# Normalized rows of an attention layer: transposed on TensorE, or loaded channel-major and normalized on GpSimd

## The chip, the cores and the metric

The kernel runs on one core of one Trainium2 chip. The metric is the time of the whole kernel on the device in microseconds (us). The engines are TensorE (PE in the profile), VectorE (DVE), ScalarE (ACT), GpSimd (POOL) and SyncE (SP, which here only starts DMAs). Each works through its own list of instructions in order and waits on semaphores for the others.

## The reference, cut to what matters

Input `x` is 128 batch items of 128 tokens by 384 channels, `adj` is 128 x 128 per item. Two layers follow each other:

```python
x = x + gnn(layernorm(x), adj, adj, ...)     # layer A: 12 heads of 32 channels
x = x + ffn(layernorm(x), ...)               # layer B: 3 heads of 128 channels

# layer A
q, k, v = h @ Wq.T, h @ Wk.T, h @ Wv.T + bv              # h = layernorm(x)
scores = q k^T * scale + 2 * adj                         # per head; rows all zero are masked
out = softmax(scores) @ v @ Wo.T + bo

# layer B
gate = softmax(relu(h @ Wg1 + bg1) @ Wg2 + bg2)          # two best of three, softmax again
q, k, v per head; q of head 0 passes a convolution over tokens (3 taps)
out = (causal softmax attention per head, weighted by the gate) @ Wp + bp
```

`layernorm(x)` is (x - mean) / sqrt(var + 1e-5) over the 384 channels of a token. The result must come close to float32, so the kernel splits each operand of the large products into two float16 parts (`hi` and `lo`) and adds three products per operand pair.

## The kernel before

The 128 items are worked in 32 groups of 4. In the main loop a *turn* holds one group of layer A (from its scores on), one group of layer B (the group before that), and, "ahead", the normalized rows and q, k of the group that layer A takes in the next turn. The turn is the same from turn 2 to turn 31. Turns 0 and 1 and the last groups have lists of their own (`FIRST_STEPS`, `LAST_STEPS`).

The order on each engine is a table, `ORDER_OF_STEPS`: for each engine a list of steps such as `A.score.1.2` (layer A, item 1, block 2 of four heads). Each engine runs its steps strictly in that order; semaphores hold the engines to each other. The steps that matter here:

- `A.ln1`: DVE computes mean and variance of the next group's rows (L807, L811), POOL turns them into -mean and 1/sqrt(var) (L1048 to L1051) and normalizes the 4 items into `h1`, tokens on partitions (L1054).
- `A.hT.c` (c = 0, 1, 2): PE transposes block c of 128 channels of the 4 items into one PSUM bank (four transposes, L560), ACT writes the float16 `hi` part from it (L677), DVE the `lo` part (L927). `A.qk.0` needs all three blocks.
- `A.score` (PE, then DVE L957, then ACT exp L712), `A.norm` (DVE row factors L974 to L982, then POOL L1096), `A.turn` (PE transposes the probabilities, ACT copies them, L726), `A.mix`, `A.proj`: layer A's attention.
- `B.qk.c` (ACT evacuates it, L701 or L704), `B.v`, `B.score`, `B.norm`, `B.turn`, `B.mix`, `B.proj`: layer B. `B.score.0` waits until ACT has evacuated `B.qk.5`.
- `B.gate.0`, `.1`, `.2`: the gate on DVE (L873 to L899), with two small exponentials on ACT (L735) between the parts. `B.gate.0` has five instructions with two inputs in SBUF: three of L875, L879, L882.
- `A.res`, `B.res`: POOL adds a bias row to the residual (L1082, L1091).
- `A.stack.0`, `.1`: SP copies q and k parts to `Qs` and `Ks` with 24 DMAs (L492). The first waits for the last scores of the group before; the next turn's first scores wait for the last.

PSUM has 8 banks: 5 used in rotation by layer A's steps, 3 by layer B's. A step on PE waits until the step that used its bank before has been evacuated.

Of the kernel before, what the change touches and what calls it, by code (L numbers as in the profile page):

```python
# [45 lines left out]
GB = 4  # L46
# [80 lines left out]
        A.score.0.0 A.score.0.1 A.v.0 A.v.1 A.score.0.2 B.hT.0 B.hT.1 B.hT.2 A.score.1.0 A.score.1.1 A.v.2  # L127
        B.qk.0 B.v.0 B.v.1 A.score.1.2 B.qk.1 B.v.2 A.turn.0.0 A.v.3 A.turn.0.1 B.v.3 B.qk.2 A.turn.0.2 B.qk.3
        A.hT.0 A.score.2.0 A.hT.1 A.mix.0 A.score.2.1 B.qk.4 A.hT.2 B.qk.5 A.turn.1.0 A.proj.0 B.score.0
        A.turn.1.1 B.score.1 A.score.2.2 A.qk.0 A.turn.1.2 A.score.3.0 A.qk.1 A.qk.2 A.qk.3 B.turn.0 A.qk.4  # L130
        B.mix.0 A.score.3.1 A.mix.1 A.score.3.2 B.turn.1 B.score.2 A.turn.2.0 A.qk.5 A.turn.2.1 A.proj.1
# [5 lines left out]
        A.score.1.1 A.turn.0.2 B.qk.2 A.hT.0 A.score.1.2 A.hT.1 B.gate.0 A.mix.0 B.qk.3 A.hT.2 B.qk.4 B.qk.5
        A.turn.1.0 A.score.2.0 A.turn.1.1 A.score.2.1 A.qk.0 B.gate.1 B.score.0 A.qk.1 A.turn.1.2 A.score.2.2
        B.score.1 A.qk.2 B.turn.0 A.qk.3 A.qk.4 A.score.3.0 B.mix.0 A.mix.1 B.turn.1 A.turn.2.0 A.score.3.1
        B.score.2 A.score.3.2 A.turn.2.1 A.turn.2.2 B.mix.1 A.qk.5 A.mix.2 B.turn.2 B.score.3 A.turn.3.0 B.mix.2  # L140
        A.turn.3.1 A.turn.3.2 B.turn.3 A.mix.3 B.mix.3
    """,
    "dve": """
        A.score.0.0 A.v.0 A.score.0.1 A.score.0.2 B.hT.0 B.hT.1 B.hT.2 A.smax.0 A.v.1 A.score.1.0 B.v.0 A.norm.0
        A.score.1.1 A.ln1 A.v.2 B.v.1 A.score.1.2 B.v.2 A.v.3 B.conv B.v.3 A.smax.1 B.gate.0 A.hT.0 A.norm.1
        A.hT.1 A.score.2.0 A.mix.0 A.hT.2 A.score.2.1 B.gate.1 B.score.0 A.proj.0 A.score.2.2 B.score.1 B.gate.2
        A.qk.0 B.norm.0 A.smax.2 A.qk.1 A.score.3.0 B.norm.1 A.norm.2 A.qk.2 A.qk.3 A.qk.4 A.score.3.1 A.mix.1
        B.score.2 A.score.3.2 B.mix.0 A.smax.3 B.norm.2 A.norm.3 B.score.3 B.mix.1 A.qk.5 A.proj.1 B.proj.0
# [1020 lines left out]
```

## Time and profile before

| what | us |
|---|---|
| three runs, median (lowest to highest) | 2238.28 (2237.51 to 2238.32) |
| the profiled execution, whole time | 2238.38 |
| its span, first to last instruction | 2236.3 |
| PE busy in the span | 2201.6 (98%) |
| DVE busy | 1903.9 (85%) |
| ACT busy | 1500.0 (67%) |
| POOL busy | 1157.3 (52%) |

Engines work at the same time, so their busy times don't add up. A time is bound by the engine that is never idle, or by a circle of waits; the share tells the first, the waits the second.

### The profile page before, as it was taken

To read this page: it belongs to the slowest core of one execution; us is meant where nothing else is said; L and a number is where in the kernel's file an instruction comes from. 1 tells how busy PE (TensorE), PEld (TensorE's weight loads), DVE (VectorE), ACT (ScalarE), POOL (GpSimd) and SP (SyncE) were. 2 spreads that over 40 slices of the span, in tenths; PEclk is the share of its full clock that TensorE was granted. 3 is DMA by queue.
4 is the path that set the end of the run, shared out by engine and by line. 5 is a ranking of instruction groups with operands and counts; after the bars stand their busy time and mean duration, and the time that the engine had idled before them with its cause. 6 is when DMAs were issued, how large, how long until landed. Compare 5 with 4: busy or idle time off the path is not lost.

```text
span 2236.3 us, 51593 instructions
## 1 busy us (share of the span) xinstructions
PE 2201.6 (98%) x16941; PEld 1439.2 (64%) x16941; DVE 1903.9 (85%) x7152; ACT 1500.0 (67%) x5298; POOL 1157.3 (52%) x1551
## 2 busy tenths in 40 slices
...
DMA packets 142265, 143.20 MB, mean 64 GB/s; under 512 B 16816, under 2 KB 141360, under 8 KB 142000
## 3 DMA queue, kind: packets, MB, share of 16 engines
...
q8 instruction: 137, 2.24, 0.4%
...
q14 instruction: 128, 1.05, 0.2%
...
## 4 chain that ended last, share of the span: by engine, by line
PE 94%; DVE 2%; SPq 1%; POOL 1%; issue 1%; DMA 0%; ACT 0%; DVEq 0%; POOLq 0%
PE B_bank L517 33%; PE A_bank L517 32%; PE A_bank L597 7%; PE A_bank L609 4%; PE B_bank L616 4%; PE A_bank L584 4%; PE B_bank L591 4%; PE B_bank L601 2%; PE A_bank L560 2%; PE B_bank L560 2%; SPq L492 1%; DVE raw_score L957 1%; DVE smax L963 0%; DMA Ks<-k_hi 0%; POOL S L1096 0%
## 5 line engine op out<-in xcount | busy, mean ns | idle before, releaser
L712 ACT ACTIVATE S<-raw_score,smin 128x128 f32<-128x128 f32 x1536 | 593.9, 393 | 172.9 <-DVE smin L957 172.9
L1096 POOL TENSOR_TENSOR S<-S,rowf 128x512 f32<-128x512 f32 x384 | 389.1, 1041 | 314.8 <-DVE rowf L982 314.8
L957 DVE CUSTOM_DVE_ANT_0 raw_score<-A_bank,adj,s_unit 128x128 f32<-128x128 f32 x1536 | 444.7, 346 | 4.3 <-PE A_bank L584 1.5
L1101 POOL TENSOR_TENSOR S<-S,row2f 128x384 f32<-128x384 f32 x128 | 106.0, 828 | 612.1 <-DVE row2f L990 611.9
L726 ACT ACTIVATE PT<-A_bank 128x512 f32<-128x512 f32 x384 | 220.1, 590 | 234.9 <-PE A_bank L597 234.9
L712 ACT ACTIVATION_READ_ACCUMULATOR S<-raw_score,smin 128x1 f32 x1536 | 296.0, 193 | 0.0
L597 PE MATMUL A_bank<-ident,S 128*128 128x128 f32 x1536 | 226.7, 274 | 3.6 <-DVE smin L957 2.5
L963 DVE TENSOR_REDUCE smax<-raw_score 128x12 f32<-128x1536 f32 x128 | 223.0, 1742 | 0.0
L597 PEld LDWEIGHTS A_bank<-ident,S 128*128 128x128 f32 x1536 | 187.0, 141 | 41.4 <-DVE smin L957 3.4
L719 ACT ACTIVATE S<-S,s2min 128x128 f32<-128x128 f32 x384 | 148.4, 390 | 3.0 <-DVE s2min L967 3.0
L584 PE MATMUL A_bank<-Ks,Qs 96*128 96x128 f16 x1536 | 140.6, 221 | 7.7 <-DMA Ks<-k_hi 5.0
L584 PEld LDWEIGHTS A_bank<-Ks,Qs 96*128 96x128 f16 x1536 | 109.1, 98 | 37.1 <-issue 12.1
L517 PE MATMUL B_bank<-wv2g_hi,b_hT_hi 128*128 128x416 f16 x384 | 130.2, 339 | 1.0 <-DVE V L946 1.0
L517 PE MATMUL B_bank<-wv2g_lo,b_hT_hi 128*128 128x416 f16 x384 | 130.2, 339 | 0.0
L517 PE MATMUL B_bank<-wv2g_hi,b_hT_lo 128*128 128x416 f16 x384 | 130.2, 339 | 0.0
L957 DVE DVE_READ_ACCUMULATOR2_ANT smin<- 128x1 f32 x1536 | 127.4, 83 | 0.0
L1091 POOL TENSOR_TENSOR x1res<-x,bp_row 128x384 f32<-128x384 f32 x128 | 125.4, 1008 | 3.0 <-DMA out<-x1res 3.0
L517 PE MATMUL A_bank<-wo_hi,oT_hi 128*128 128x384 f16 x384 | 125.2, 326 | 1.8 <-DVE oT_lo L938 1.8
L517 PE MATMUL B_bank<-wp_hi,yT_hi 128*128 128x384 f16 x384 | 125.2, 326 | 1.6 <-DVE yT_lo L938 1.5
L1082 POOL TENSOR_TENSOR xres<-xin,bo_row 128x384 f32<-128x384 f32 x128 | 125.7, 1015 | 0.0
L517 PE MATMUL A_bank<-wv_hi,a_hT_hi 128*128 128x384 f16 x384 | 125.3, 326 | 0.0
L517 PE MATMUL B_bank<-wp_hi,yT_lo 128*128 128x384 f16 x384 | 125.2, 326 | 0.0
(192 smaller groups left out, 6155.8 us busy)
## 6 DMA issues: line engine op xcount, KB each, us to landing
xin<-in_x SPq DMA_DIRECT2D x32, 768.0 KB, 4.5
...
out<-x1res SPq DMA_DIRECT2D x128, 192.0 KB, 2.1
...
Qs<-q_lo SPq DMA_DIRECT2D x128, 96.0 KB, 2.2
Ks<-k_lo SPq DMA_DIRECT2D x126, 96.0 KB, 2.3
...
```

Of the source, the lines that this page charges most:

```text
L517: mm = nc.tensor.matmul(dst, left(c)[a], right(c)[b], start=(c == 0 and n == 0), stop=(c == KC - 1 and n == 2))
L584: mm = nc.tensor.matmul(dst[:, tok(j)], Qs[:, c * HPC + j, tok(b)], Ks[:, c * HPC + j, tok(b)], start=True, stop=True)
L597: mm = nc.tensor.transpose(dst[:, tok(j)], S[b % 2][:, c * HPC + j, :], ident[:])
L712: ins = nc.scalar.activation(S[b % 2][:, h, :], raw_score[:, h, :], ACT.Exp, bias=smin[b % 2][:, h:h + 1], scale=-1.0, accum_out=ssum[b % ...
L719: ins = nc.scalar.activation(S2[b % 2][:, e, :], S2[b % 2][:, e, :], ACT.Exp, bias=s2min[b % 2][:, e:e + 1], scale=-1.0, accum_out=s2sum[b ...
L726: nc.scalar.activation(dst, src[:, 0:dst.shape[1]], ACT.Copy).then_inc(evacuated[stage, "act"], 1)
L957: ins = nc.vector.tensor_tensor_reduce(raw_score[:, h, :], src[:, j * T:(j + 1) * T], adj2[:, b, :], s_unit[:], 3.0e38, ALU.add, ALU.min, ...
L963: nc.vector.tensor_reduce(smax[b % 2][:], raw_score[:], AXX, ALU.max).then_inc(maxed, 1)
L1082: nc.gpsimd.tensor_tensor(xres[:, b, :], xin[:, b, :], bo_row[:], ALU.add).then_inc(xres_ready, 1)
L1091: nc.gpsimd.tensor_tensor(x1res[:, b, :], x1[:, b, :], bp_row[:], ALU.add).then_inc(x1res_ready, 1)
L1096: nc.gpsimd.tensor_tensor(S[b % 2][:, hs, :], S[b % 2][:, hs, :], rowf[b % 2][:, hs].unsqueeze(2).broadcast_to([P, HPC, T]), ALU.mult).the ...
L1101: nc.gpsimd.tensor_tensor(S2[b % 2][:], S2[b % 2][:], row2f[b % 2][:].unsqueeze(2).broadcast_to([P, NE, T]), ALU.mult).then_inc(normed2, 1)
```

## The change

The host hands over a second copy of `x`, already channel-major (`xT`: group, channel in block, block, item and token). From group 2 on (`TURNED`):

- SP loads a group's `xT` into `xt` (`A.xT`, 768 KB). `xt` takes the place of `h1`.
- POOL computes -mean and 1/sqrt(var) as before (now `A.ln1` is only that), but these lie one token per partition. SP writes them to DRAM as rows (`A.stat`: 128 partitions x 8 values, each of 4 bytes to a place of its own) and reads them back to all 128 partitions (`A.rows`: `stat_wide`, 128 x 1024).
- POOL normalizes block c with two instructions of 128 x 512 (`A.hx.c`): add -mean, multiply by 1/sqrt(var).
- ACT and DVE read `xt` in SBUF instead of a PSUM bank to write the `hi` and `lo` parts. PE has no `A.hT` steps.

Groups 0 and 1 are transposed as before. The tables of the main loop are new for all five engines.

```diff
+                if (stage, kind) == ("A", "xT") and not last:
+                    if following(g) == TURNED:
+                        wait_products(sp, ("A", "hT", KC - 1, 0), g)
+                    else:
+                        wait_evacuated(sp, ("A", "hT", KC - 1, 0), g)
+                    sp.dma_start(xt[:], xT[following(g)]).then_inc(xT_loaded, 16)
+                if (stage, kind) == ("A", "stat"):
+                    sp.wait_ge(rstd1_done, count(g, 1, 1))
+                    sp.dma_start(stat_rows[g].rearrange("q b t -> t q b"), stat[g % 2][:],
+                                 allow_slow_non_contiguous=True).then_inc(stat_stored, 16)
+                if (stage, kind) == ("A", "rows"):
+                    sp.wait_ge(stat_stored, count(g - TURNED, 16, 16))
+                    if g > TURNED:
+                        sp.wait_ge(hx_ready, count(g - TURNED, KC, 0))
+                    sp.dma_start(stat_wide[:], stat_rows[g].rearrange("q b t -> q (b t)").unsqueeze(0)
+                                 .broadcast_to([P, 2, GB * T])).then_inc(stat_spread, 16)
...
+                elif kind == "hT" and A and g >= TURNED:
+                    act.wait_ge(hx_ready, count(g - TURNED, KC, b + 1))
+                    if b == 0:
+                        wait_products(act, ("A", "v", GB - 1, 0), before(g))
+                        wait_products(act, ("A", "qk", 2 * KC - 1, 0), before(g))
+                    nc.scalar.activation(hT_hi["A"][:, b, :], xt[:, b, :], ACT.Copy, scale=H_SCALE)\
+                        .then_inc(hi_ready["ahead"], 1)
...
-                    nc.vector.scalar_tensor_tensor(out=hT_lo[stage][:, b, :], in0=src[:, :], scalar=H_SCALE,
+                    rows_T = xt[:, b, :] if turned(step, g) else src[:, :]
+                    nc.vector.scalar_tensor_tensor(out=hT_lo[stage][:, b, :], in0=rows_T, scalar=H_SCALE,
...
+                elif kind == "hx":
+                    if b == 0:
+                        pool.wait_ge(xT_loaded, count(g - TURNED, 16, 16))
+                        pool.wait_ge(stat_spread, count(g - TURNED, 16, 16))
+                    nc.gpsimd.tensor_tensor(xt[:, b, :], xt[:, b, :], stat_wide[:, 0, :], ALU.add).then_inc(centred, 1)
+                    pool.wait_ge(centred, count(g - TURNED, KC, b + 1))
+                    nc.gpsimd.tensor_tensor(xt[:, b, :], xt[:, b, :], stat_wide[:, 1, :],
+                                            ALU.mult).then_inc(hx_ready, 1)
```

Of the new tables, PE's up to `A.qk.0` and POOL's:

```diff
     "pe": """
+        A.score.0.0 A.v.0 A.score.0.1 A.v.1 A.score.0.2 A.score.1.0 B.hT.0 B.hT.1 B.hT.2 A.v.2 B.qk.0
+        A.score.1.1 A.score.1.2 B.qk.1 B.v.0 A.turn.0.0 A.turn.0.1 B.v.1 B.qk.2 A.turn.0.2 B.v.2 A.mix.0 A.v.3
+        B.v.3 A.score.2.0 B.qk.3 A.turn.1.0 A.turn.1.1 A.score.2.1 A.turn.1.2 B.qk.4 B.qk.5 A.score.2.2 A.proj.0
+        B.score.0 A.mix.1 B.score.1 A.qk.0 A.qk.1 A.score.3.0 A.qk.2 A.qk.3 B.turn.0 A.score.3.1 B.score.2
...
     "pool": """
+        A.res.0 A.res.1 A.res.2 A.res.3 B.res.0 A.norm.0 A.ln1 A.norm.1 B.res.1 A.hx.0 A.hx.1 A.hx.2 B.norm.0
+        A.norm.2 B.norm.1 B.res.2 B.norm.2 A.norm.3 B.res.3 B.norm.3 A.ln2.0 A.ln2.1 A.adj A.ln2.2 A.ln2.3
```

POOL's list in a turn, from the residual rows of layer A to the norm of layer B's first item, before:

```order
L1082 TENSOR_TENSOR xres<-xin,bo_row 128x384 x4
L1096 TENSOR_TENSOR S<-S,rowf 128x512 x3
L1048 TENSOR_SCALAR nmean<-mv 128x4
L1049 TENSOR_SCALAR ve<-mv 128x4
L1051 TENSOR_TENSOR rstd<-ve,half 128x4
L1054 TENSOR_SCALAR h<-xin,nmean,rstd 128x384 x4
L1091 TENSOR_TENSOR x1res<-x,bp_row 128x384 x4
```

The same stretch now:

```order
L1138 TENSOR_TENSOR S<-S,rowf 128x512 x3
L1133 TENSOR_TENSOR x1res<-x,bp_row 128x384
L1168 TENSOR_TENSOR xt<-xt,stat_wide 128x512
L1170 TENSOR_TENSOR xt<-xt,stat_wide 128x512
L1168 TENSOR_TENSOR xt<-xt,stat_wide 128x512
L1170 TENSOR_TENSOR xt<-xt,stat_wide 128x512
L1168 TENSOR_TENSOR xt<-xt,stat_wide 128x512
L1170 TENSOR_TENSOR xt<-xt,stat_wide 128x512
L1143 TENSOR_TENSOR S<-S,row2f 128x384
```

Before, four normalizations (L1054) and four residual rows (L1091) stood in one run, ahead of `A.norm.1`. Now `A.norm.1` (L1138 x3) and one residual row come first, and then the six `A.hx` instructions in one run, ahead of `B.norm.0`.

ACT's list in the middle of a turn, where the gate's first exponential (L735) stands, before:

```order
L677 ACTIVATE a_hT_hi<-A_bank 128x512
L712 ACTIVATE S,ssum<-raw_score,smin 128x128 x4
L677 ACTIVATE a_hT_hi<-A_bank 128x512
L735 ACTIVATE g_tmp<-g_tmp 128x12
L730 ACTIVATE oT_hi<-A_bank 128x384
L704 ACTIVATE k<-B_bank,bqk_col,hinv 128x512
L677 ACTIVATE a_hT_hi<-A_bank 128x512
L704 ACTIVATE k<-B_bank,bqk_col,hinv 128x512 x2
```

The same stretch now (the gate's exponential is L769):

```order
L746 ACTIVATE S,ssum<-raw_score,smin 128x128 x4
L769 ACTIVATE g_tmp<-g_tmp 128x12
L707 ACTIVATE a_hT_hi<-xt 128x512
L738 ACTIVATE k<-B_bank,bqk_col,hinv 128x512
L760 ACTIVATE PT<-A_bank 128x512 x2
L738 ACTIVATE k<-B_bank,bqk_col,hinv 128x512
L746 ACTIVATE S,ssum<-raw_score,smin 128x128 x4
L707 ACTIVATE a_hT_hi<-xt 128x512 x2
```

Two evacuations of `B.qk` (L738), `.4` and `.5`, and two of `A.turn.1` (L760) now stand behind both the gate's exponential and the first block of `A.hT`.

DVE's list there now, from the last two `B.v` to the first block of `A.hT`; each `ISA` row is one of four alike:

```order
L981 SCALAR_TENSOR_TENSOR V<-B_bank,v_unit,bvg_row 128x416 x2
L992 ISA raw_score,smin<-A_bank,adj,s_unit 128x128
...
L907 TENSOR_SCALAR g_hid<-V 128x128
L909 TENSOR_TENSOR q2raw<-g_hid,wg_row 128x128 x3
L912 TENSOR_REDUCE g_tmp<-q2raw 128x12
L913 TENSOR_TENSOR g_tmp<-g_tmp,bg_row 128x12
L914 TENSOR_REDUCE g_col<-g_tmp 128x4
L916 TENSOR_TENSOR g_tmp<-g_tmp,g_col 128x12
...
L962 SCALAR_TENSOR_TENSOR a_hT_lo<-xt,a_hT_hi 128x512
```

`B.gate.0` (L907 to L916) has the same instructions as before; it follows `A.score.2.0` now, where it followed `A.smax.1`, and the two-input form of `A.hT` (L962) comes behind it, later in the list.

## Rows read from the trace of the kernel before

**Rows 1.** The page: span; part 1: busy us, share, instructions.

```profile
span 2236.3 us, 51593 instructions
PE 2201.6 (98%) x16941; PEld 1439.2 (64%) x16941; DVE 1903.9 (85%) x7152; ACT 1500.0 (67%) x5298; POOL 1157.3 (52%) x1551
```

**Rows 2.** Windows: one turn; PE, PEld, DVE, ACT, POOL busy; PEclk.

```profile
607.19:675.36 68.17, 68.17 (x530) 44.68 (x528) 58.86 (x223) 46.36 (x166) 35.67 (x48) 1.00 0.24 63
```

**Rows 3.** Chain of waits by time: start, us, engine, tile, matmuls.

```profile
638.13 1.32 PE B_bank L560 x12
646.47 0.23 PE A_bank L584 x4
650.66 1.46 PE A_bank L517 x9
652.56 3.52 PE B_bank L517 x18
...
658.46 0.44 PE A_bank L560 x4
659.57 0.79 PE A_bank L609 x24
...
671.52 5.83 PE A_bank L517 x27
```

**Rows 4.** Timeline of PE and POOL: start, us, instruction.

```profile
634.37 0.61 PE L584 MATMUL A_bank<-Ks,Qs 96*128 96x128 f16 x8
...
650.35 1.04 POOL L1051 TENSOR_TENSOR rstd<-ve,half 128x4 f32<-128x4 f32 x1
```

**Rows 5.** Groups by line, POOL: busy us, mean ns | idle before.

```profile
L1096 POOL TENSOR_TENSOR S<-S,rowf 128x512 f32<-128x512 f32 x384 | 389.1, 1041 | 314.8 <-DVE rowf L982 314.8
L1082 POOL TENSOR_TENSOR xres<-xin,bo_row 128x384 f32<-128x384 f32 x128 | 125.7, 1015 | 0.0
L1054 POOL TENSOR_SCALAR h<-xin,nmean,rstd 128x384 f32<-128x384 f32 x126 | 112.2, 902 | 3.5
```

**Rows 6.** Lines L875 and L979: min/median/max ns, first and last start.

```profile
L875 DVE TENSOR_TENSOR q2raw<-g_hid,wg_row x9: 278/991/1082, 657.1 to 795.4; 128x128 f32<-128x128 f32 x9
L979 DVE SCALAR_TENSOR_TENSOR live<-smax,live x128: 105/107/671, 52.2 to 2173.7; 128x12 f32<-128x12 f32 x128
```

**Rows 7.** Timeline of POOL, then DVE, around the gate's first part.

```profile
655.03 3.92 POOL L1091 TENSOR_TENSOR x1res<-x,bp_row 128x384 f32<-128x384 f32 x4
...
657.10 2.20 DVE L875 TENSOR_TENSOR q2raw<-g_hid,wg_row 128x128 f32<-128x128 f32 x3
...
660.33 0.17 DVE L882 TENSOR_TENSOR g_tmp<-g_tmp,g_col 128x12 f32<-128x12 f32 x1
```

**Rows 8.** Groups by line, ACT and DVE.

```profile
L712 ACT ACTIVATE S<-raw_score,smin 128x128 f32<-128x128 f32 x1536 | 593.9, 393 | 172.9 <-DVE smin L957 172.9
L726 ACT ACTIVATE PT<-A_bank 128x512 f32<-128x512 f32 x384 | 220.1, 590 | 234.9 <-PE A_bank L597 234.9
L704 ACT ACTIVATE k<-B_bank,bqk_col,hinv 128x512 f32<-128x512 f32 x96 | 74.1, 773 | 24.0 <-PE B_bank L517 24.0
L677 ACT ACTIVATE a_hT_hi<-A_bank 128x512 f16<-128x512 f32 x96 | 56.5, 589 | 54.4 <-PE A_bank L560 54.4
...
L957 DVE CUSTOM_DVE_ANT_0 raw_score<-A_bank,adj,s_unit 128x128 f32<-128x128 f32 x1536 | 444.7, 346 | 4.3 <-PE A_bank L584 1.5 <-DVE smax L963 0.3
L946 DVE SCALAR_TENSOR_TENSOR V<-B_bank,v_unit,bvg_row 128x416 f32<-128x416 f32 x128 | 82.4, 644 | 19.4 <-PE B_bank L517 19.4
```

**Rows 9.** Timeline of SP, another turn: start, us of issuing.

```profile
1158.93 6.43 SPq L492 DMA_DIRECT2D Qs<-q_hi  x8
...
1173.83 3.99 SPq L492 DMA_DIRECT2D Ks<-k_hi  x4
```

**Rows 10.** Part 6 of the page: KB each, us to landing.

```profile
xin<-in_x SPq DMA_DIRECT2D x32, 768.0 KB, 4.5
...
out<-x1res SPq DMA_DIRECT2D x128, 192.0 KB, 2.1
```

More of the change, by code:

```diff
@@ L126 @@
     "pe": """
[L127 to L131, printed above, removed]
@@ L137 @@
[L137 to L141, printed above, removed]
+        A.score.0.0 B.hT.0 B.hT.1 B.hT.2 A.score.0.1 A.score.0.2 B.qk.0 A.score.1.0 B.qk.1 A.turn.0.0 A.turn.0.1
@@ new lines @@
+        A.score.1.1 A.turn.0.2 B.qk.2 A.score.1.2 A.mix.0 A.turn.1.0 B.qk.3 A.score.2.0 B.gate.0 A.hT.0 B.qk.4
+        A.turn.1.1 A.turn.1.2 B.qk.5 A.score.2.1 A.hT.1 A.hT.2 A.mix.1 B.gate.1 B.score.0 A.qk.0 A.qk.1
+        A.score.2.2 B.score.1 B.turn.0 A.qk.2 A.qk.3 A.score.3.0 B.mix.0 A.turn.2.0 B.score.2 A.score.3.1 A.qk.4
+        A.score.3.2 B.turn.1 A.turn.2.1 A.qk.5 A.turn.2.2 B.mix.1 B.turn.2 B.score.3 A.turn.3.0 A.mix.2
+        A.turn.3.1 A.turn.3.2 B.mix.2 A.mix.3 B.turn.3 B.mix.3
@@ L142 @@
     """,
     "dve": """
[L144 to L148, printed above, removed]
@@ L149 @@
-        A.mix.2 B.norm.3 A.ln2.0 B.proj.1 A.ln2.1 B.mix.2 A.proj.2 A.mix.3 A.ln2.2 B.mix.3 B.proj.2 A.proj.3
-        A.ln2.3 B.proj.3
+        A.score.0.0 A.v.0 A.score.0.1 A.v.1 A.score.0.2 B.hT.0 B.hT.1 B.hT.2 A.smax.0 A.v.2 A.norm.0 A.score.1.0
+        A.ln1 A.score.1.1 A.score.1.2 B.v.0 B.v.1 A.smax.1 B.conv A.norm.1 A.mix.0 A.v.3 B.v.2 B.v.3 A.score.2.0
+        B.gate.0 A.score.2.1 B.gate.1 A.score.2.2 A.hT.0 A.proj.0 A.hT.1 A.hT.2 B.score.0 B.gate.2 A.mix.1
+        A.smax.2 B.score.1 B.norm.0 A.qk.0 A.norm.2 A.qk.1 A.score.3.0 A.qk.2 B.score.2 A.qk.3 B.norm.1
@@ L151 @@
+        A.score.3.1 A.score.3.2 B.norm.2 B.mix.0 A.smax.3 A.qk.4 A.norm.3 B.score.3 A.qk.5 B.proj.0 B.mix.1
+        A.proj.1 B.norm.3 A.ln2.0 A.mix.2 B.mix.2 A.ln2.1 B.proj.1 A.mix.3 A.proj.2 A.ln2.2 B.mix.3 A.proj.3
+        A.ln2.3 B.proj.2 B.proj.3
     """,
     "pool": """
-        A.res.0 A.res.1 A.res.2 A.res.3 A.norm.0 A.ln1 B.res.0 B.res.1 B.res.2 B.res.3 A.norm.1 B.norm.0
-        B.norm.1 A.norm.2 B.norm.2 A.norm.3 B.norm.3 A.ln2.0 A.ln2.1 A.adj A.ln2.2 A.ln2.3
+        A.res.0 A.res.1 A.res.2 A.res.3 B.res.0 A.norm.0 A.ln1 A.norm.1 B.res.1 A.hx.0 A.hx.1 A.hx.2 B.norm.0
@@ L206, with turned @@
 }
+def turned(step, g):
+    return step[:2] == ("A", "hT") and g >= TURNED
 def parse(word):
```

61 lines of the change are left out of this document (38 added, 23 removed).

## The prediction, written before the changed kernel was run

> **What bounds the kernel now.** I read the page's busy shares first: PE 98%, the next engine 85% [rows 1]. Then windows one turn long: in a window of 68.17 us PE is busy for 68.17 us at the full granted clock (2.4 GHz), DVE for 58.86, ACT for 46.36, POOL for 35.67 [rows 2]. So in a turn the time is what PE issues, and only less PE work, or a new wait of PE, can change it. The chain of waits says the same: it is one PE step behind another.
>
> **What goes.** Three A.hT steps a turn. In the chain one of them (four transposes) moves PE on by 0.44 us [rows 3]. They go for groups 2 to 31, 30 turns: 3 x 0.44 = 1.32 us a turn, 39.6 us in all. POOL loses four normalizations of 0.90 us a turn [rows 5], 3.6 us, off the path, since POOL is 52% busy [rows 1].
>
> **What comes, away from the path.** POOL gets six two-input instructions of 128 x 512 a turn. The trace has no such form with two full operands. Nearest rows: 1.04 us for 512 elements with a broadcast operand, 1.01 us for 384 elements with full operands [rows 5], which go at a step of 3.92 / 4 = 0.98 us [rows 7]. Scaled to 512 elements that is 1.31 us. Below: 1.04 + 0.1 for the own semaphore between the two of a block, 1.15. Above: 1.35 + 0.1 = 1.45. I take 1.3, so a block of 7.8 us. POOL's load rises by 4 us to about 40 of 68 us: it is not the bound. ACT and DVE keep their three A.hT instructions each, from SBUF instead of PSUM; I price them as before, 0.59 us on ACT [rows 8].
>
> **The new order, laid out.** I add up PE's steps from the turn's first score. Step costs: scores 0.23, B.hT all three 1.32, A.v and A.proj 1.46, qk 5.83 / 3 = 1.94, B.v 3.52 - 1.94 = 1.58, A.turn 0.44 (four transposes, as A.hT), A.mix 0.79 and 0.1 in front of it [rows 3]. Up to B.score.0 the new list has 9 scores, 4 A.v, B.hT, 6 B.qk, 4 B.v, 6 A.turn, one A.mix, one A.proj: 2.07 + 5.84 + 1.32 + 11.64 + 6.32 + 2.64 + 0.89 + 1.46 = 32.2 us. B.v.3 ends at 22.9, the third A.turn.0 at 17.3, A.qk.0 starts at 34.4 (B.score.0, A.mix.1 and B.score.1 add 2.2). These are the times if PE never waits.
>
> *When POOL starts the block.* ACT copies A.turn.0.2 (0.59), evacuates B.qk.2 (0.77) and does the four exponentials of A.score.1.2 (4 x 0.39) [rows 8]; less overlaps that is 17.5 to 20.3. DVE needs about 0.5 for the row factors (four short instructions, L979 is 0.11 when alone [rows 6]), POOL 3 x 1.0 for A.norm.1 and 1.0 for a residual row [rows 5]: the first A.hx can start at 25.0.
>
> *When DVE does the gate.* B.v.3 read from 23.1, 0.6 us; A.score.2.0, four of 0.35 that overlap, 1.1 us [rows 8]: B.gate.0 starts at 24.7. It took from 656.7, just ahead of 657.10, to 660.50 before [rows 7], 3.8 us. It would end at 28.5.
>
> So the gate's first part and the six A.hx run side by side, and that is the point of this prediction. L875 takes 278 ns at the least and 991 in the middle of nine [rows 6]. In the timeline POOL works through four L1091 until 658.95, and the three L875 that began at 657.10 took 2.20 us: each ended with a POOL instruction, only the third, when POOL was done, was short [rows 7]. L979, 105 ns, has been 671 [rows 6]. A DVE instruction with two SBUF inputs is held until POOL's running instruction ends. [...] Without such a rule this layout would give the clean case below; with it, what follows.
>
> B.gate.0 has five such instructions. They can each get in only at the end of an A.hx: ends at 26.3, 27.6, 28.9, 30.2, 31.5. So B.gate.0 ends at 31.7 instead of 28.5. ACT stands at the gate's exponential, and behind it in its list are A.hT.0, B.qk.4, two A.turn.1, B.qk.5: 0.59 + 0.77 + 2 x 0.59 + 0.77 = 3.3 us by the means [rows 8], about 3.0 as they overlap. B.qk.5 is evacuated at 34.7. PE wants B.score.0 at 32.2 and waits 2.5 us. Without the holds it would be 31.5, ahead of 32.2 by 0.7. A.qk.0 then comes at 36.9 and finds its first blocks (DVE reaches A.hT.0 near 35.5, having done A.score.2.1, the gate's second part and A.score.2.2); little is added there.
>
> Bounds of this wait: with 1.15 us an instruction the fifth end is at 30.8, less overlap on ACT, wait 1.5; with 1.45 it is 32.3, wait 3.2. If the block starts later than 25.0, the first part of the gate goes free, but its second part and A.hT.1 and .2 meet the block, which ends later itself: from a start at 28.5 it ends at 36.3, ACT and DVE add 1.3, and A.qk.0 wants its last block at 35.7: a wait of about 2. So it doesn't vanish by a shift.
>
> **The moments' way.** -mean and 1/sqrt(var) were ready 17.0 us into a turn (650.35 + 1.04 against 634.37 [rows 4]); A.ln1 now stands ahead of A.score.1.1 on DVE, so some 2 us earlier, 15. Until 25.0 there are 10 us for two dependent DMAs. A store of 192 KB lands in 2.1 us, a load of 768 KB in 4.5 [rows 10]. For the 1024 values of 4 bytes no row exists: below 2.1, above twice the 4.5 (xin is 512 pieces, this is 1024), 9. With 4.5 for the way back the pair takes 6.6 to 13.5; I take 9, hidden. The loads and SP's part in them lie far from the stacking in time.
>
> **The stacking.** The Q and K copies start when PE has done A.score.3.2 and must have landed before the next turn's first score. In a turn that is slow at it they took from 1158.93 to 1177.82 to issue [rows 9], 18.9 us (the longest of the 13 turns that I read; the shortest took 16.8), and some 1.5 to land (2.1 from the start of an issue, as for the stores [rows 10]). PE's list had 20.9 us between the two, now 19.8. A wait of up to 0.7 us in the slowest turns, two of those 13: 3 us over all, counted in.
>
> **Sum.** The profiled execution took 2238.38 us (span 2236.3, 2.1 around it), 0.1 above the median of the runs, so I count from 2238. A turn: -1.32 + 2.5 = +1.2 us. Thirty turns: +35. Stacking +3. Forecast 2276 us, slower. Its own range: 30 x (1.5 - 1.32) = +5 to 30 x (3.2 - 1.32) + 3 = +59: 2243 to 2298.
>
> **Rivals.**
> - *Clean.* The gate and the block don't meet as I laid them, or the lists have slack that I don't see, and PE stays 100% busy: 2238 - 39.6 + 3 = 2201 us, faster. For it: in the turn before, DVE was held by 1.4 us in the same gate and PE never waited [rows 2, 7]. Against it: that had some microseconds of other ACT work between, now ACT stands right behind the gate and PE's margin is 0.7. It decides at this point: if five holds cost less than 0.7 us together.
> - *Half.* The holds cost 1 to 1.5 us beyond the margin less what later steps win back: 30 x (1.2 - 1.32) = -4, 2220 to 2243 us. For it: my layout has an error of some tenths at each engine.
> - *The moments come late.* The 4-byte stores pass 10 us with the read. Each microsecond past it is a microsecond a turn once the wait for A.hT.2 leads: at 15 us for the pair the block starts at 30, ends at 37.8, its last block is ready at 39.1 against 35.7: +3.4 - 1.32 a turn, 2300; at 20 us 2450. For it, the Trainium skill (DMA: Bandwidth & Descriptors, "Specifications") wants 512 B and more for the full rate and has smaller pieces read, changed and written back; no row here has pieces of 4 bytes in number. Against: it is 4 KB in all over 16 DMA engines.
>
> **Chances.** Forecast 0.50, clean 0.33, half 0.10, late moments 0.07. What can be told from no change is about 0.2%, 4.5 us. Of half, 0.03 is faster by more than that, 0.01 slower by more, 0.06 within. So slower 0.50 + 0.07 + 0.01 = 0.58, faster 0.33 + 0.03 = 0.36, within 0.06. The range for 8 in 10 must hold the clean case too: 2198 to 2298.
>
> **What would show it.** In the changed profile, a window of one turn: PE's busy time near 67 in a turn of 69.4 (forecast) or of 66.9 (clean). PE's longest waits: B_bank of B.score.0, released by ACT's evacuation into k (forecast), or a_hT_lo from DVE or the stat_wide load (late moments). L909 (L875 before) with a median near 1.3 us and L913, L916 far above their 0.17: holds. The A.hx pair at 1.15 to 1.45 us each. ACT idle in front of the gate's exponential by about 3 us. Wrong at the root: L909 short, or the six A.hx finished before or begun after the gate, with PE fully busy.

## The result, and the profile after

The changed kernel took 2322.23 us, the median of four runs (2320.09 to 2324.97), against 2238.30 of the kernel before on the same chip (2237.51 to 2240.0): a ratio of 1.0375, interval 1.0357 to 1.0393. The profiled execution took 2324.97 us. So it is slower, as forecast, but by 84 us where 38 were forecast, and outside the range of 2198 to 2298.

The page of the changed kernel, its span, part 1 and the start of part 4 (the chain's shares); it answers to [rows 1]:

```profile
span 2323.2 us, 51084 instructions
...
PE 2210.8 (95%) x16581; PEld 1418.0 (61%) x16581; DVE 1899.8 (82%) x7152; ACT 1488.3 (64%) x5298; POOL 1285.9 (55%) x1611
...
PE 49%; DMA 18%; DVE 17%; POOL 6%; issue 5%; ACT 4%; SPq 1%; ACTq 0%; DVEq 0%; POOLq 0%
```

PE has 360 matmuls fewer and is busy 9 us longer than in [rows 1]. Of the chain, DMA now has 18%. The waits of the changed kernel (engine, tile and line waiting <- releaser: us in total, times, longest):

```profile
POOL xt L1168 <- DMA stat_wide<-stat_rows: 122.9, 30, 5.4
ACT a_hT_hi L707 <- POOL xt L1170: 110.8, 60, 4.5
...
PE B_bank L618 <- ACT k L738: 75.3, 31, 3.8
```

PE's wait stands exactly where it was forecast, at B.score.0 behind ACT's evacuation of B.qk.5, and its size, 75.3 / 30 = 2.5 us a turn, is the forecast's. Its cause is another. The timeline of one turn, which starts at 736.10 (SP's DMA issues, POOL and ACT, start and us; idle time before an instruction in brackets):

```profile
749.66 1.04 POOL L1090 TENSOR_TENSOR stat<-ve,half 128x4 f32<-128x4 f32 x1
750.73 0.38 SPq L498 DMA_DIRECT2D stat_rows<-stat  x1
...
761.00 0.34 SPq L505 DMA_DIRECT2D stat_wide<-stat_rows  x1
...
764.09 0.21 ACT L769 ACTIVATE g_tmp<-g_tmp 128x12 f32<-128x12 f32 x1
...
765.34 1.27 POOL L1168 TENSOR_TENSOR xt<-xt,stat_wide 128x512 f32<-128x512 f32 x1 [4.62 <-DMA stat_wide<-stat_rows]
...
767.98 0.63 ACT L707 ACTIVATE a_hT_hi<-xt 128x512 f16<-128x512 f32 x1 [3.69 <-POOL xt L1170]
...
770.14 0.79 ACT L738 ACTIVATE k<-B_bank,bqk_col,hinv 128x512 f32<-128x512 f32 x1
...
771.02 0.91 PE L618 MATMUL B_bank<-k,q 128*128 128x128 f32 x6 [3.00 <-ACT k L738]
```

The moments are ready 14.6 us into the turn. The store is issued at once, and the spread, which waits for it, only 10.3 us later; it lands after 4.2 us more. Over all 30 turns the first step takes 8.2 to 11.2 us (median 10.0) and the second 3.4 to 5.3 (median 4.5). POOL was free at 24.6 and starts the block at 29.2. ACT has done the gate's exponential at 764.3 and stands in front of A.hT.0 until the first block is done; B.qk.4 and B.qk.5 are queued behind it, and PE waits for the latter (the L738 row at 770.14).

The gate's first part had slipped through ahead of the block. L909, its three products, and L921, an instruction of the gate's second part (min/median/max ns; L909 answers to L875 in [rows 6]):

```profile
L909 DVE TENSOR_TENSOR q2raw<-g_hid,wg_row x96: 278/285/1121, 117.0 to 2293.4; 128x128 f32<-128x128 f32 x96
...
L921 DVE TENSOR_TENSOR g_tmp<-g_tmp,g_col x32: 170/809/1266, 120.9 to 2299.2; 128x12 f32<-128x12 f32 x32
```

L909 at a median of 285 ns is free; the second part, beside the block now, is held (L921, a median of 809 ns against 170 at the least). And there is a second cost. Windows of the same turn (start:end, length, busy of PE, PEld, DVE, ACT and POOL with instructions, granted clock, DMA share, GB/s), then the 4 us behind a wait of 2.91 us in the turn before and behind one of 1.98 us in the turn after:

```profile
736.10:807.87 71.77, 68.77 (x518) 44.02 (x517) 57.75 (x223) 45.99 (x165) 40.00 (x51) 0.98 0.29 78
768.00:771.00 3.00, 0.03 (x1) 0.01 (x1) 1.60 (x2) 3.00 (x6) 2.92 (x3) 1.00 0.00 0
771.00:773.00 2.00, 1.98 (x31) 1.50 (x31) 0.00 (x0) 1.97 (x9) 1.92 (x2) 0.85 0.00 0
773.00:775.00 2.00, 2.00 (x8) 1.52 (x9) 1.85 (x5) 1.11 (x3) 0.43 (x1) 0.50 0.00 0
775.00:777.00 2.00, 2.00 (x9) 0.80 (x8) 1.79 (x13) 1.26 (x6) 0.00 (x0) 0.80 0.00 0
...
698.00:702.00 4.00, 4.00 (x34) 3.33 (x35) 1.87 (x5) 3.17 (x12) 2.33 (x2) 0.50 0.00 0
841.80:845.80 4.00, 3.98 (x43) 2.57 (x44) 1.91 (x5) 3.02 (x12) 2.34 (x2) 1.00 0.00 0
```

Behind 22 of the 30 waits at B.score.0 the granted clock is 0.50 to 0.67 over the next 4 us, which is some microseconds at the 1.2 GHz level, and the matmuls take up to twice their time; behind the other 8 it is 1.00. PE is busy 68.77 us in the turn shown, where the layout had 66.9.

### The profile page after: what moved, and what is told of

Its sections match the earlier page's. It is cut to its first block, busy times and chain, and to the rows that moved or that the text cites. A ratio compares the mean times of both kernels' runs of the same rounds, so it can differ in the third digit from the quotient of the medians.

```text
span 2323.2 us, 51084 instructions
## 1 busy us (share of the span) xinstructions
PE 2210.8 (95%) x16581; PEld 1418.0 (61%) x16581; DVE 1899.8 (82%) x7152; ACT 1488.3 (64%) x5298; POOL 1285.9 (55%) x1611
## 4 chain that ended last, share of the span: by engine, by line
PE 49%; DMA 18%; DVE 17%; POOL 6%; issue 5%; ACT 4%; SPq 1%; ACTq 0%; DVEq 0%; POOLq 0%
PE A_bank L544 22%; DMA stat_rows<-stat 11%; PE B_bank L544 8%; DVE raw_score L992 6%; DMA stat_wide<-stat_rows 6%; PE B_bank L618 5%; PE A_bank L624 4%; PE B_bank L643 4%; PE A_bank L636 4%; DVE smax L998 3%; DVE bn L841 2%; DVE b_hT_lo L962 2%; ACT k L738 2%; PE B_bank L628 2%; POOL xt L1170 2%
## 5 line engine op out<-in xcount | busy, mean ns | idle before, releaser
L1138 POOL TENSOR_TENSOR S<-S,rowf 128x512 f32<-128x512 f32 x384 | 389.5, 1043 | 456.4 <-DVE rowf L1017 456.4
L992 DVE CUSTOM_DVE_ANT_0 raw_score<-A_bank,adj,s_unit 128x128 f32<-128x128 f32 x1536 | 439.6, 345 | 15.1 <-PE A_bank L611 14.5
L760 ACT ACTIVATE PT<-A_bank 128x512 f32<-128x512 f32 x384 | 217.6, 592 | 234.3 <-PE A_bank L624 234.3
L746 ACT ACTIVATION_READ_ACCUMULATOR S<-raw_score,smin 128x1 f32 x1536 | 301.9, 197 | 0.0
L624 PE MATMUL A_bank<-ident,S 128*128 128x128 f32 x1536 | 218.7, 275 | 3.6 <-DVE smin L992 2.5
L618 PE MATMUL B_bank<-k,q 128*128 128x128 f32 x768 | 132.6, 316 | 75.3 <-ACT k L738 75.3
L624 PEld LDWEIGHTS A_bank<-ident,S 128*128 128x128 f32 x1536 | 179.4, 142 | 36.3 <-issue 8.5
L1168 POOL TENSOR_TENSOR xt<-xt,stat_wide 128x512 f32<-128x512 f32 x90 | 114.5, 1272 | 122.9 <-DMA stat_wide<-stat_rows 122.9
L618 PEld LDWEIGHTS B_bank<-k,q 128*128 128x128 f32 x768 | 111.8, 219 | 97.0 <-ACT k L738 86.5
L962 DVE SCALAR_TENSOR_TENSOR a_hT_lo<-xt,a_hT_hi 128x512 f16<-128x512 f32 x90 | 75.9, 843 | 97.4 <-ACT a_hT_hi L707 93.2
L1170 POOL TENSOR_TENSOR xt<-xt,stat_wide 128x512 f32<-128x512 f32 x90 | 124.4, 1382 | 7.1
L707 ACT ACTIVATE a_hT_hi<-xt 128x512 f16<-128x512 f32 x90 | 56.6, 629 | 110.8 <-POOL xt L1170 110.8
```

The source lines that it names most:

```text
L618: mm = nc.tensor.matmul(dst[:, tok(e)], q2[:, e, tok(b)], k2[:, e, tok(b)], start=True, stop=True)
L624: mm = nc.tensor.transpose(dst[:, tok(j)], S[b % 2][:, c * HPC + j, :], ident[:])
L746: ins = nc.scalar.activation(S[b % 2][:, h, :], raw_score[:, h, :], ACT.Exp, bias=smin[b % 2][:, h:h + 1], scale=-1.0, accum_out=ssum[b % ...
L760: nc.scalar.activation(dst, src[:, 0:dst.shape[1]], ACT.Copy).then_inc(evacuated[stage, "act"], 1)
L992: ins = nc.vector.tensor_tensor_reduce(raw_score[:, h, :], src[:, j * T:(j + 1) * T], adj2[:, b, :], s_unit[:], 3.0e38, ALU.add, ALU.min, ...
L1138: nc.gpsimd.tensor_tensor(S[b % 2][:, hs, :], S[b % 2][:, hs, :], rowf[b % 2][:, hs].unsqueeze(2).broadcast_to([P, HPC, T]), ALU.mult).the ...
```

## The experiments

Eleven kernels ran. All times are against the kernel before on the same chip (2237.8 to 2238.5). The runs "no store", "narrow", "both" and "half" leave out part of the computation, as the text recorded ahead of each says, and show only what the time would be; the others compute the whole.

**The moments early: no store.**

```diff
-  sp.dma_start(stat_rows[g].rearrange("q b t -> t q b"), stat[g % 2][:], ...).then_inc(stat_stored, 16)
-  sp.wait_ge(stat_stored, count(g - TURNED, 16, 16))
-  sp.dma_start(stat_wide[:], stat_rows[g]. ...)
+  sp.dma_start(stat_wide[:], x[g * GB].rearrange("t c -> (t c)")[0:2 * GB * T]. ...)
```

> Left out: the store of the moments to DRAM; the load into stat_wide reads as many bytes of x instead, so layer A's rows are not normalized rightly. The load is issued when 1/sqrt(var) is done, 14.6 us into a turn, and lands at about 19, so the A.hx block starts when POOL is free, 24.7 to 25. Theory L (the lateness of the moments made the 2.4 us wait and the block itself is harmless): PE's wait at B.score.0 is gone and the time is the clean case, about 2201 us. Theory H (my forecast: the block held the five two-input instructions of B.gate.0): now the block really runs beside gate.0 and the wait is 2.5 us by the holds, the median of L909 near 1.1 us, time about 2276 us. In between (2215 to 2255) both have a part.

Measured: 2246.6 us, ratio 1.0034 (1.0020 to 1.0049). Neither theory alone. PE's longest wait:

```profile
PE B_bank L616 <- ACT k L736: 37.8, 31, 1.6
```

The gate's products, ns:

```profile
L907 DVE TENSOR_TENSOR q2raw<-g_hid,wg_row x96: 276/1261/1362, 114.2 to 2214.1; 128x128 f32<-128x128 f32 x96
```

And the timeline of POOL, DVE, ACT and PE in a turn from 705.99:

```profile
730.73 0.35 DVE L905 TENSOR_SCALAR g_hid<-V 128x128 f32<-128x128 f32 x1
...
730.96 1.27 POOL L1164 TENSOR_TENSOR xt<-xt,stat_wide 128x512 f32<-128x512 f32 x1
...
731.12 2.76 DVE L907 TENSOR_TENSOR q2raw<-g_hid,wg_row 128x128 f32<-128x128 f32 x3
...
732.32 1.41 POOL L1166 TENSOR_TENSOR xt<-xt,stat_wide 128x512 f32<-128x512 f32 x1
...
733.69 1.32 POOL L1164 TENSOR_TENSOR xt<-xt,stat_wide 128x512 f32<-128x512 f32 x1
...
734.50 0.53 DVE L911 TENSOR_TENSOR g_tmp<-g_tmp,bg_row 128x12 f32<-128x12 f32 x1
...
735.08 1.27 POOL L1166 TENSOR_TENSOR xt<-xt,stat_wide 128x512 f32<-128x512 f32 x1
...
735.26 1.11 DVE L914 TENSOR_TENSOR g_tmp<-g_tmp,g_col 128x12 f32<-128x12 f32 x1
...
736.41 0.21 ACT L767 ACTIVATE g_tmp<-g_tmp 128x12 f32<-128x12 f32 x1 [1.93 <-DVE g_tmp L914]
...
739.55 0.91 PE L616 MATMUL B_bank<-k,q 128*128 128x128 f32 x6 [1.22 <-ACT k L736]
```

This is the turn that the prediction laid out. The block starts 25.0 us in and the gate 24.7, as forecast; PE wants B.score.0 at 739.55 - 1.22 - 705.99 = 32.3, forecast 32.2. The products' median is 1261 ns and L911 and L914 each end with a POOL instruction: the holds are real. They cost less than forecast: the gate ends at 736.37, 30.4 us in, not 31.7, for one of the three products got in free between two that were held (2.76 us for the three; the first took 1.27 and the last 1.36), so there are four holds and not five. The wait is 1.2 us a turn, and the granted clock is 1.00 over the 4 us behind every one of them.

**The moments stored as they lie.**

```diff
-  stat_rows[g].rearrange("q b t -> t q b"), stat[g % 2][:]   (1024 pieces of 4 bytes)
+  stat_rows[g], stat[g % 2][:]                               (128 pieces of 32 bytes)
-  xt[:, b, :], stat_wide[:, 0, :]
+  rows_T, stat_wide[:, :, 0, :].rearrange("p t b -> p b t")
```

> The whole computation. The moments are stored as they lie, 128 pieces of 32 bytes instead of 1024 of 4, and the GpSimd instructions of A.hx read them from stat_wide at a step of 32 bytes. Theory P (the store takes its 9 to 10 us because of its many pieces): the store lands in about 2 us as the 192 KB output stores do, stat_wide lands near 21.5 us into the turn, the block starts at 25 as in e1, and the time is that of e1 within 10 us. Rival Q (the store is slow because it is small and scattered over rows, not because of their number): the store still takes 8 us or more, block at 28 to 29, time 2310 to 2325. Side effect: if the 32-byte step slows the tensor_tensor past 1.27 us, the block is longer and the time lies up to 30 us above e1.

Measured: 2303.5 us, 1.0292 (1.0276 to 1.0307). Theory P is right on the store: the next DMA is issued 1.42 us behind it (below). The time is not that of the run without the store but 57 us above it, where I had allowed 30 for the side effect. POOL's instruction, PE's wait, and the 4 us behind it in three turns:

```profile
L1168 POOL TENSOR_TENSOR xt<-xt,stat_wide x90: 1513/1530/1568, 112.8 to 2158.9; 128x512 f32<-128x512 f32 x90
```

```profile
PE B_bank L617 <- ACT k L737: 67.8, 31, 2.6
```

```profile
614.70:618.70 4.00, 4.00 (x44) 2.84 (x45) 4.00 (x19) 2.94 (x12) 0.00 (x0) 1.00 0.01 4
684.70:688.70 4.00, 3.98 (x37) 3.31 (x38) 4.00 (x20) 3.07 (x12) 0.00 (x0) 0.58 0.00 0
...
826.50:830.50 4.00, 4.00 (x39) 3.04 (x40) 4.00 (x19) 2.94 (x12) 0.00 (x0) 0.69 0.00 0
```

POOL's instruction takes 1.53 us instead of 1.27, each hold is so much longer, and the wait nearly doubles, to 2.2 us a turn. Even with 1.53 us an instruction PE's wait is below the 2.5 that I forecast for 1.3. The clock falls again: over the 4 us behind the wait it is 0.57 to 0.69 in 18 turns and 1.00 in the other 12, and the waits are 2.20 to 2.23 us in 29 of the 30. So of the 57 us, 30 are more waiting and 28 are more time for the same matmuls (PE busy 2199.1, against 2171.2 in the run without the store). The Trainium skill (GPSIMD Engine Reference, "Performance pitfalls for Q7 kernels") says that a read with a step over 8 bytes costs about half as much again. The trace agrees in kind, with 20% for a step of 32 bytes in one operand of two, and with 2% for a step of 8 bytes (1.30 us, in the run with the pairs below).

**Narrow: A.hx on 8 columns, all DMAs kept.**

```diff
-  nc.gpsimd.tensor_tensor(xt[:, b, :], xt[:, b, :], stat_wide[:, 0, :], ALU.add)
+  nc.gpsimd.tensor_tensor(xt[:, b, 0:8], xt[:, b, 0:8], stat_wide[:, 0, 0:8], ALU.add)
```

(and the product likewise)

> Left out: A.hx works on 8 of 512 columns of each block, so most rows of layer A stay unnormalized; all DMAs as in the changed kernel. stat_wide still lands at 29 us into the turn, the six instructions then take some 0.1 to 0.2 us each, so A.hT.0 can start at 29.5 instead of 31.9. Theory L: ACT's wait in front of A.hT.0 falls from 3.7 to 1.3 us, PE's wait at B.score.0 from 2.4 to 0.3 or less, the clock stays full, time 2201 to 2215. Theory H says the same 2201 for another reason (no holds); what tells them apart is e1. A third theory, that the time is lost elsewhere (more DMA traffic, clock), has it stay above 2250.

Measured: 2221.1 us, 0.9922 (0.9907 to 0.9936), PE's wait 13.8 us in 19 places. The DMA is as late as ever:

```profile
POOL xt L1168 <- DMA stat_wide<-stat_rows: 125.1, 30, 5.3
```

With the block's length gone, 0.5 us a turn of it reaches PE, a little more than the 0.3 of theory L, and the time is 6 us above its range. The wait and PE's busy time account for it (the table below); nothing is left over for the added DMA traffic as such.

**Both: the floor of the new order.** The edits of the first and the third together.

> Left out: the store of the moments, as in the run without the store, and A.hx works on 8 of 512 columns, as in the narrow run. So the moments are early and nothing holds DVE beside the gate: the floor of the new order. The run without the store took 2246.6 with a wait of 1.2 us a turn at B.score.0 and a median of 1261 ns for the gate's three products. Theory H2 (with early moments the whole rest of that wait is the holds): here the products are back at 0.28 us, the wait at B.score.0 is under 0.1 us a turn and the time 2238 - 39.6 + up to 9 for the start and the stacking, 2200 to 2209. Rival: the wait comes from the lists of ACT and DVE themselves (too much ahead of B.qk.5), then 0.5 us or more a turn stays, 2215 or more.

Measured: 2202.4 us, 0.9841 (0.9827 to 0.9856), no wait at B.score.0, products at 290 ns, PE busy 2165.5. Theory H2 holds. The forecast's clean case, 2201, is within 1 us of this floor, but by two errors that cancel: the +3 for stacking in it does not show (PE waits 5.7 us for Ks here, 5.0 in the kernel before), and PE's busy time falls by 36.1 us, not 39.6.

**A.hT.0 later in ACT's list.**

```diff
-  B.gate.0 A.hT.0 B.qk.4 A.turn.1.1 A.turn.1.2 B.qk.5 A.score.2.1 A.hT.1
+  B.gate.0 B.qk.4 A.turn.1.1 A.turn.1.2 B.qk.5 A.score.2.1 A.hT.0 A.hT.1
```

> The changed kernel with one step moved in ACT's list: A.hT.0 stands behind B.qk.5 and A.score.2.1, where B.score.0 doesn't wait for it. The moments stay late, the block ends 37.3 us into the turn. Theory L (late moments): the 2.4 us at B.score.0 go, but A.qk.0 wants the third block at about 35.7 and has it at 38.8, so a wait of 2 to 3 us appears at A.qk.0, released by DVE's a_hT_lo: the wait moves, time 2290 to 2325. Rival (only the place of A.hT.0 in ACT's list was wrong): the wait is gone altogether, 2205 to 2225.

Measured: 2352.3 us, 1.0513 (1.0497 to 1.0529). The wait moves to A.qk.0 as theory L has it (PE's wait, then a window around it in one turn):

```profile
PE A_bank L544 <- DVE a_hT_lo L962: 89.3, 70, 2.0
```

```profile
783.50:791.50 8.00, 6.03 (x23) 2.39 (x24) 5.94 (x25) 3.57 (x12) 1.64 (x2) 0.79 0.00 0
```

3.0 us a turn, at the upper end. The total is 27 us above what I gave: PE is now busy 2226.5 us, 61 more than the floor, which the range had no term for. In the turn of the window two waits, of 1.90 and 1.69 us, end 2.5 us apart, and the granted clock is 0.79 over the 8 us from 783.5. Late moments can't be hidden by moving one step of ACT.

**Fillers: PE works through the wait.**

```diff
                     if b == 0:
+                        for _ in range(10):
+                            nc.tensor.matmul(dst[:, :], WQ2[0][:, 0, 0:P], hT_hi["B"][:, 0, :], start=True, stop=True)
                         wait_evacuated(pe, ("B", "qk", 2 * KC - 1, 0), g)
```

> The changed kernel with ten more f16 matmuls (128x512, 0.216 us each, 2.16 us in all) in front of B.score.0's wait, into the bank that B.score.0 overwrites: PE works through most of the 2.4 us instead of standing. Theory C (some 40 us of the changed kernel's 84 are matmuls at the lower granted clock behind the wait; its PE is busy 2210.8 us for the same work that takes 2171 in the run without the store): the clock stays full, PE's busy time less the 67 us of fillers is about 2171, the time falls by 30 to 40 to 2282 to 2295 although PE has more to do. Rival (the clock costs nothing on the path): 2322 or, with the fillers longer than some waits, 2322 to 2340.

Measured: 2295.5 us, 1.0259 (1.0243 to 1.0274): 27 us less than the changed kernel, with 69 us of matmuls more.

```profile
PE 2245.6 (98%) x16901; PEld 1420.9 (62%) x16901; DVE 1898.7 (83%) x7152; ACT 1485.4 (65%) x5298; POOL 1287.1 (56%) x1611
```

```profile
ACT a_hT_hi L709 <- POOL xt L1172: 114.5, 60, 4.2
...
PE B_bank L620 <- ACT k L740: 12.9, 18, 1.3
```

Less the fillers (320 x 0.216 = 69.1) PE is busy 2176.5 us instead of 2210.8. ACT still waits 114.5 us for POOL in front of A.hT, as in the changed kernel. Behind the longest of the waits that are left, 0.8 to 1.3 us, the clock is 1.00. So 34 of the 45 us by which PE's busy time exceeded the floor went when PE no longer stood. The fillers and the wait that is left are 82.0 us, 6.7 more than the old wait; 34.3 less for the other matmuls makes 27.6 less, and 26.7 were measured. Theory C holds, at the upper end of its range: the slower matmuls are a cost of the wait, not of the change's own work.

**The moments one turn ahead.** Beside the loads below, A.ln1 takes the moments of group g + 2, and SP stores, spreads and loads xT for the next turn.

```diff
-  sp.dma_start(xin[:], dram_group(x, following(g))).then_inc(x_loaded, 16)
+  sp.dma_start(xin[:], dram_group(x, g + 2)).then_inc(x_loaded, 16)            (after A.res)
+  sp.wait_ge(stats1, count(g + 2, 1, 1))
+  sp.dma_start(xin[:], dram_group(x, following(g))).then_inc(x_loaded, 16)     (after its moments)
 POOL
-  B.res.0 A.norm.0 A.ln1 A.norm.1 B.res.1 A.hx.0 A.hx.1 A.hx.2 B.norm.0
+  B.res.0 A.hx.0.0 A.hx.0.1 A.hx.1.0 A.norm.0 A.lnx A.hx.1.1 A.hx.2.0 A.hx.2.1 A.norm.1 B.res.1 B.norm.0
 SP
-  A.res A.stat A.rows A.stack.0 A.adj A.stack.1 B.proj.0 B.proj.1 B.proj.2 B.proj.3 A.xT
+  A.res A.again A.stat A.rows A.xT A.stack.0 A.adj A.stack.1 B.proj.0 B.proj.1 B.proj.2 B.proj.3
```

> The whole computation, the moments one turn ahead: x of the next but one group is loaded into xin after A.res, its moments taken, and x of the next group loaded again for A.res (768 KB more a turn); store and spread then have a turn's time, xT is loaded as soon as A.hT.2 has left xt, and the A.hx block is cut: three instructions in POOL's idle stretch before A.norm.0 (5.5 to 9.5 us into the turn), three between the moments and A.norm.1 (15 to 20.8). The store keeps its 1024 pieces. Theory L, and H too, since nothing meets the gate: PE busy 100%, a turn of 66.9 us, 2201 us. Rival: the instructions now hold DVE's row factors of A.norm.0 and A.norm.1 or push A.norm on POOL, and PE waits at A.turn.0.0 or A.turn.1.0: each 0.1 us a turn is 3 us, up to 1 us a turn, 2231. A second rival: the second load of x and the spread beside the stacking delay it: waits at the turn's first score, 1 us a turn.

Measured: 2211.8 us, 0.9880 (0.9866 to 0.9895), with the slow store in it. No wait at B.score.0; one of 8.6 us at the first full turn, so the last step was to take A.lnx and the DMAs for group 2 earlier in the lists of the first turns (`FIRST_STEPS`) of DVE, POOL and SP:

> The whole computation: the version with the moments one turn ahead (2211.8), with the steps of the first turns in another order, since 8.6 us of its waits came once, at the first full turn, where the store of group 2's moments waited behind the stacking and landed 13 us late: its moments are taken after A.norm.1 of the first group and stored before the second stacking. Expected: that wait gone, 2203 +- 3 us. Rival: it only moves to another step of the first turns, 2208 to 2212.

Measured: 2204.7 us, 0.9852 (0.9836 to 0.9869), the best version, 33 us below the kernel before. One turn of it:

```profile
736.00:802.90 66.90, 66.90 (x518) 43.25 (x516) 57.53 (x223) 45.70 (x165) 39.58 (x51) 1.00 0.38 96
```

PE is busy for all of 66.90 us; the layout gave 68.17 - 1.32 = 66.85. Both rivals stay out: the six instructions hold nothing that PE waits for (the gate's products are back at 285 ns), and 768 KB more a turn cost at most the 2.3 us by which this kernel is above the floor. Two things that matter changed together here: the moments came a turn earlier and the block left the gate. The run without the store had only the first, and took 2246.6: the early moments alone would not have made the change faster.

**What makes the store slow.** Three kernels with other pieces. First, pairs:

```diff
-  stat = [sb(f"stat{k}", [P, 2, GB]) ...]
+  stat = [sb(f"stat{k}", [P, GB, 2]) ...]
-  stat_rows[g].rearrange("q b t -> t q b"), stat[g % 2][:]
+  stat_rows[g].rearrange("b t q -> t b q"), stat[g % 2][:]
...
```

> The whole computation. The two moments of a row lie side by side, so the store has 512 pieces of 8 bytes for the same 4 KB; A.hx reads stat_wide at a step of 8 bytes. Measured so far: 1024 pieces of 4 bytes some 10 us, 128 pieces of 32 bytes 1.4 us. Theory N (the store's time goes with the number of pieces, 8.6 us for 896 pieces more): 1.4 + 384 x 9.6 ns = 5.1 us, stat_wide lands 14.7 + 5.1 + 3.6 = 23.4 us into the turn, before POOL is free at 24.9, so the gate's products are held (median above 1.2 us) and the time is 2247 if the 8-byte step is free on POOL, up to 2304 if it costs as the 32-byte step did. Rival S (pieces below some size are slow however many): 8 us or more, the block starts at 27 or later, products near 0.28 us, time 2300 to 2325.

Measured: 2248.2 us, 1.0047 (1.0024 to 1.0070), products at 1281 ns. The time is N's, its straight line is not: the store takes 2.8 to 4.7 us over the 30 turns (median 3.8) where it gave 5.1. This is the whole computation with one thing changed, the pieces of the store, and 74 us of the 84 are gone: the late moments are what made the changed kernel slow. What is left above the floor is in the main the wait at B.score.0 behind the holds, 40.1 us. To see whether it is the number of the pieces or their size, two more:

```diff
 half: one moment alone, 512 pieces of 4 bytes
+  sp.dma_start(stat_rows[g][1].rearrange("b t -> t b"), stat[g % 2][:, 1, :], ...)
 twice: 1024 pieces of 8 bytes
+  stat = [sb(f"stat{k}", [P, 2 * GB, 2]) ...]; stat_rows: (NG, 2 * GB, T, 2)
```

> Measured: a store of 1024 pieces of 4 bytes takes 9 to 10 us until the next DMA can be issued behind it, 512 pieces of 8 bytes 2.9 us, 128 pieces of 32 bytes 1.4 us. So their number alone doesn't set it in a straight line. Left out here: the mean is not stored (the row of it in stat_wide holds values of x from one load), so layer A's rows are not normalized rightly; the store has 512 pieces of 4 bytes. Theory B (a 4-byte piece costs more than an 8-byte one): 1.4 us fixed and 8.5 ns a piece, so 5 us or more for 512. Theory K (the number sets it, but costs more than in proportion at 1024): 2.9 us as with 512 pieces of 8 bytes.

> The whole computation; the store of 512 pieces of 8 bytes is widened to 1024 pieces of 8 bytes (the second half zeros that nobody reads), all else as in that run (2248). Theory B: pieces of 8 bytes are cheap, the store takes about 4.4 us (1.4 + twice 1.5), stat_wide lands 22.7 us into the turn, time 2248. Theory K: 9 us as with 1024 pieces of 4 bytes, the block starts at 28.5, 2300 to 2320.

Measured, one run each: 2304.5 and 2247.7 us. The SP timelines, store and the spread that waits for it, of the kernels with 128 x 32 bytes, 512 x 8, 1024 x 8 and 512 x 4 in this order (the changed kernel's, 1024 x 4, is above):

```profile
736.09 0.33 SPq L498 DMA_DIRECT2D stat_rows<-stat  x1
737.51 0.33 SPq L504 DMA_DIRECT2D stat_wide<-stat_rows  x1
```

```profile
723.07 0.38 SPq L498 DMA_DIRECT2D stat_rows<-stat  x1
725.94 0.34 SPq L505 DMA_DIRECT2D stat_wide<-stat_rows  x1
```

```profile
721.35 0.38 SPq L498 DMA_DIRECT2D stat_rows<-stat  x1
725.92 0.34 SPq L505 DMA_DIRECT2D stat_wide<-stat_rows  x1
```

```profile
739.44 0.38 SPq L501 DMA_DIRECT2D stat_rows<-stat  x1
747.64 0.34 SPq L508 DMA_DIRECT2D stat_wide<-stat_rows  x1
```

1.4, 2.9, 4.6 and 8.2 us in these turns. Over all 30 turns, lowest to highest and median:

| store | us until the spread is issued |
|---|---|
| 128 x 32 bytes | 1.4 to 1.8, 1.4 |
| 512 x 8 bytes | 2.8 to 4.7, 3.8 |
| 1024 x 8 bytes | 4.3 to 5.1, 4.6 |
| 512 x 4 bytes | 8.2 to 11.1, 8.6 |
| 1024 x 4 bytes (changed kernel) | 8.2 to 11.2, 10.0 |

Half as many pieces of 4 bytes save only 1.4 us in the median, while twice as many pieces of 8 bytes still take 4.6. Theory B is right that the 4 bytes do it; its straight line, 5 us for 512 of them, was too low. Why a piece of 4 bytes is so much slower than one of 8 stays open.

## Why the prediction was wrong, step by step

One sum accounts for every run to 3 us: the floor 2202.4, plus PE's wait at the disputed place, plus PE's busy time above the floor's 2165.5.

| kernel | wait | busy above floor | sum | measured |
|---|---|---|---|---|
| changed | 75.3 | 45.3 | 2323.0 | 2322.2 |
| no store | 37.8 | 5.7 | 2245.9 | 2246.6 |
| packed | 67.8 | 33.6 | 2303.8 | 2303.5 |
| narrow | 13.8 | 5.4 | 2221.6 | 2221.1 |
| A.hT.0 later | 89.3 | 61.0 | 2352.7 | 2352.3 |
| fillers | 12.9 | 80.1, of it 69.1 fillers | 2295.4 | 2295.5 |
| moments ahead, first | 9.6 (at A.turn, 8.6 of it once) | -0.6 | 2211.4 | 2211.8 |
| moments ahead, best | 0 | -0.1 | 2202.3 | 2204.7 |
| pairs | 40.1 | 8.5 | 2251.0 | 2248.2 |
| half | 65.7 | 37.1 | 2305.2 | 2304.5 |
| twice | 39.9 | 5.7 | 2248.0 | 2247.7 |

Two steps of the prediction failed. One is the path: the moments were taken as hidden, and they come late. The other is the size: the matmuls behind the wait were priced at the full clock. The first changes what the wait is made of, but at the same total; the second is what put the number outside the range.

- *What goes, 1.32 us a turn:* nearly right. The best version's turn is 66.90 us, and PE's busy time falls by 36.1 us in all at the floor, where I had 39.6.
- *The layout:* right to 0.4 us at each point that could be checked: POOL free at 24.6 (25.0), gate at 24.7, B.score.0 wanted at 32.3 (32.2), moments ready at 14.6 (15).
- *The moments' way: the step of the path that failed.* "I take 9, hidden." It took 14.6 in the turn shown: 10.3 until the spread was issued and 4.2 more. I had set the store's upper bound at 9, which most turns pass, and took the pair near the middle of 6.6 to 13.5. My own upper end put the block's start at 15 + 13.5 = 28.5, past the 25.0 of the cover. I had worked out that very start, as a wait of about 2 us, and concluded only that the wait would not vanish; neither the forecast nor its chances used it. The rival got 0.07, with 2300 for a pair of 15 us. It was the case that came, 22 us longer than that.
- *Its price was wrong as well.* I had late moments arrive at PE through the last block and A.qk.0. They arrive through the first: A.hT.0 stands in ACT's list ahead of B.qk.4 and B.qk.5, so B.score.0 waits. I had written that very queue down for the gate and didn't use it for the block. The run with A.hT.0 moved shows the path that I had priced. The rival's wait, 3.4 us a turn for a block at 30, was above the 2.5 measured for one at 29.2; what it lacked was the clock.
- *The holds, 2.5 us a turn:* the mechanism is right where it applies (products at 1261 ns with the store gone), but in the changed kernel the gate is through before the block. Where it applies the term was mis-sized: four holds, 1.2 us, below my lower bound of 1.5. Forecast and result agree in the place of the wait and in its size only by chance; without the experiment the 2.5 us would have passed for a proof.
- *The A.hx instruction, 1.3 us:* 1.27 measured.
- *Stacking, +3:* not there.
- *The clock: the step of the size that failed.* No term in the sum; a wait was priced at its own length, at nothing beyond it, and no reason was given. PE's busy time above the floor is 45 us. The fillers show 34 of these directly; 5.7 stand above the floor in the run without the store too, with the clock at 1.00 behind every wait, so those are not shown to be the clock's. With the terms at their measured size, 2238 - 36 + 75 + 45 gives the result. The terms that the prediction had measure -36 + 75 = +39 together, where it had -40 + 75 + 3 = +38, so almost all of the 46 us between forecast and result is this term. It would have been missing had the holds been as large as forecast too: the run with packed moments has holds, a wait of 2.2 us a turn, and 33.6 us of PE busy above the floor.
